# A gated delta rule in a four-stage program: decays scanned on VectorE, keys scaled on ScalarE, query norms folded into gating

## What is computed

```python
def step(S, inp):
    qt, kt, vt, gt, bt = inp
    S = S * jnp.exp(gt)
    delta = (vt - kt @ S) * bt
    S = S + kt[:, None] * delta[None, :]
    return (S, qt @ S)
...
q = short_conv(hidden_states @ Wq, conv_wq)
k = short_conv(hidden_states @ Wk, conv_wk)
q = l2norm(q.reshape(B, T, H, -1))
k = l2norm(k.reshape(B, T, H, -1))
beta = jax.nn.sigmoid(hidden_states @ Wb)
g = -jnp.exp(A_log) * jax.nn.softplus(hidden_states @ Wa + dt_bias)
o = gated_delta_rule(q, k, v, g, beta)
o_n = o * jax.lax.rsqrt(jnp.mean(o * o, axis=-1, keepdims=True) + NORM_EPS) * norm_w
o_n = o_n * jax.nn.silu(gg)
```

## Time and profile before

| | us |
|---|---|
| median of three runs | 1908.83 (1908.02 to 1911.7) |
| the profiled execution | 1907.61 |
| its span, first to last instruction | 1905.7 |
| delta rule within it | about 822 to 1644 |

### The profile page before, as it was taken

How to read it: one execution, slowest core, us unless ns; L and a number is a source line. 1 busy time by engine, 2 the same in 40 slices (tenths; PEclk the granted TensorE clock), 3 DMA queues, 4 the chain that set the end, 5 groups by cost and what they waited for, 6 DMA issues and landing times. The chain is left out here.

```text
span 1905.7 us, 27790 instructions
## 1 busy us (share of the span) xinstructions
PE 1526.6 (80%) x10592; PEld 1026.1 (54%) x10666; DVE 1038.4 (54%) x2369; ACT 665.9 (35%) x1185; POOL 693.8 (36%) x1097
## 2 busy tenths in 40 slices
PE   4787787777959996758799999999999996387782
PEld 3354554444536664324565676657666675365562
DVE  3856556455223553746467666777668542155553
ACT  3062251431612222544344544454444521022112
POOL 3020110300000000016778777787768672111343
PEclk8999899898979997989899999999999976598896
DMA  1000000000030003230231223222331211421355
GB/s 54 1 1 1 23 2 1 23 1 1 13 90 12 23 22 109 83 67 17 40 56 23 42 48 57 43 36 34 56 56 26 37 29 28 126 95 56 79 116 143
DMA packets 216902, 84.33 MB, mean 44 GB/s; under 512 B 166265, under 2 KB 211682, under 8 KB 216770
## 3 DMA queue, kind: packets, MB, share of 16 engines
q1 hardware_dynamic: 205330, 68.10, 16.1%
q0 software_dynamic: 5376, 12.59, 2.5%
q10 hardware_dynamic: 6064, 1.86, 0.4%
HBM read 50.80 MB, written 31.72 MB: 43 GB/s over the span
## 5 line engine op out<-in xcount | busy, mean ns | idle before, releaser
L1806 DVE SCALAR_TENSOR_TENSOR d_conv<-d_prep,k_cw,d_conv 128x511 f32<-128x511 f32 (+2 forms) x288 | 214.3, 746 | 32.1 <-ACT d_conv L1637 25.3
L1758 POOL TENSOR_TENSOR d_prod<-d_blk 64x30 f32<-64x30 f32 (+4 forms) x360 | 173.4, 482 | 102.9 <-DMA d_blk<-mid_a_blk 75.6
L1427 PE MATMUL d_prep<-k_hT,k_w 128*128 128x512 f32 x384 | 190.7, 621 | 24.4 <-POOL d_power L1732 12.7
L1762 POOL TENSOR_TENSOR d_blk<-d_blk,d_prod 64x30 f32<-64x30 f32 (+4 forms) x360 | 183.4, 509 | 28.2
L424 ACT ACTIVATE a_probs<-a_acc 128x896 f32<-128x896 f32 x128 | 117.1, 918 | 173.7 <-PE a_acc L248 110.7
L523 DVE TENSOR_REDUCE a_top<-a_turn 128x4 f32<-128x512 f32 (+3 forms) x240 | 147.5, 652 | 48.2 <-PE a_turn L210 40.4
L471 POOL TENSOR_TENSOR a_rstd<-a_rstd,a_mhalf 128x4 f32<-128x4 f32 x4 | 4.1, 1027 | 368.8 <-DVE a_rstd L575 368.8
L1427 PEld LDWEIGHTS d_prep<-k_hT,k_w 128*128 128x128 f32 x384 | 68.4, 198 | 85.6 <-issue 48.8
L1637 ACT ACTIVATE d_conv<-d_prep,k_cw 128x512 f32<-128x512 f32 x96 | 66.0, 687 | 132.6 <-PE d_prep L1427 132.4
L1465 PE MATMUL d_prep<-d_kq 128*128 128x256 f32 x384 | 94.7, 391 | 15.8 <-DVE d_qkT L1838 15.1
L1465 PEld LDWEIGHTS d_prep<-d_kq 128*128 128x128 f32 x384 | 72.8, 197 | 44.6 <-DVE d_qkT L1838 26.9
(11 more groups left out here) (356 smaller groups left out, 3522.5 us busy)
## 6 DMA issues: line engine op xcount, KB each, us to landing
mid_gate<-p_gate SPq DMA_DIRECT2D x4, 768.0 KB, 3.4
mid_v<-p_v_tok SPq DMA_DIRECT2D x4, 768.0 KB, 3.7
d_v_h<-mid_v SPq DMA_DIRECT2D x12, 256.0 KB, 5.6
d_gate_h<-mid_gate SPq DMA_DIRECT2D x12, 256.0 KB, 5.4
mid_a_blk<-d_AT SPq DMA_DIRECT2D x48, 64.0 KB, 2.0
d_blk<-mid_a_blk SPq DMA_DIRECT2D x12, 256.0 KB, 3.6
mid_u_blk<-d_blk SPq DMA_DIRECT2D x12, 256.0 KB, 2.9
mid_l_blk<-d_blkT SPq DMA_DIRECT2D x12, 256.0 KB, 3.7
```

The costliest lines, as they stand in the source:

```text
L1427: last = nc.tensor.matmul(PB[f % 2][:], w[:, n % 2, i, k, :], hT[:, k, b * T:(b + 1) * T], start=k == 0, stop=k == CK - 1)
L1758: nc.gpsimd.tensor_tensor(pr, blk[:, 0:t, t:t + 1].broadcast_to([lanes, t, m]), blk[:, t:t + 1, t + 1:BLK].broadcast_to([lanes, t, m]), AL ...
L1762: nc.gpsimd.tensor_tensor(blk[:, 0:t, t + 1:BLK], blk[:, 0:t, t + 1:BLK], pr, ALU.subtract).then_inc(subst, 1)
L1806: ins = nc.vector.scalar_tensor_tensor(dst, PB[f % 2][:, 0:T - j], cw[:, n % 2, f % 2, TAPS - 1 - j:TAPS - j], dst, ALU.mult, ALU.add)
```

## The change

- The decays from position to position are no longer made by matmuls and Exp. With exp(g) of each position, alpha, in a row, a scan along the row gives the running products: out[t] = out[t-1] x alpha[t] + diag[t], where `diag` is 1 on the diagonal and alpha is 0 at the first position of each chunk (which ends the row before). The projections turn g over on TensorE, raise it (`alpha_ready`) and store it; `load_decays` (SyncE) loads 512 alphas of one head and batch, the same row for all 128 partitions; `scan_decays` (VectorE) scans it in place, in the recurrence two heads ahead. `spread`, `differences`, `decay_up` and their constants and buffers go.
- `keep_keys` is on ScalarE, 16 copies of 128x128 with the decay as scale.
- The multiply by the query norms goes: mean(o^2) + eps |q|^2 takes the place of mean((o/|q|)^2) + eps, with `eps_q` made in `scales`. `raise_norms` has 16 columns instead of 32.
- The forming stands wholly ahead of the inversion on VectorE, queries first (`weigh_queries` of tiles 0 and 1 before the norms). On TensorE `turn_out` and `correlate(q, 0)` stand ahead of `sum_squares(q, 1)`. On ScalarE the last `keep_out` of a head stands ahead of the last Silu of the head two later. `scale_values` stands ahead of `finish`.
- `gate_h` has two buffers and its own load, later in SyncE's queue.

```diff
@@ layer1_projections @@
+                    if b - 2 == BATCH - 1:
+                        sp.wait_ge(alpha_ready, 1)
+                        sp.dma_start(d["alpha"].rearrange("(a r) t -> r a t", a=2), alpha[:]).then_inc(alpha_out, 16)
                     store_values(b - 2)
...
+            for a in range(2):
+                last = nc.tensor.transpose(GB[1][0:n // 2, 2 * P + a * P:2 * P + (a + 1) * P],
+                                           g[:].rearrange("p h t -> p (h t)")[:, a * (n // 2):(a + 1) * (n // 2)], ident[:])
             last.then_inc(summed, 1)
...
+            nc.scalar.activation(alpha[:, :, 1:P], GB[1][0:n // 2, 2 * P:4 * P].rearrange("r (a t) -> r a t", a=2)[:, :, 1:P], ACT.Exp).then_inc(alpha_ready, 1)
@@ layer1_delta_rule, SyncE @@
+            def load_decays(n, some):
+                for b in some:
+                    if n:
+                        sp.wait_ge(attn, 8 * n - 8 + 2 * b + 2)
+                    sp.dma_start(alpha[:, b, :], alpha_d[n:n + 1, b, :].broadcast_to([P, T])).then_inc(alpha_in[b], 16)
...
                 if n + 1 < D_H:
                     gather_blocks(n + 1)
+                if n + 3 < D_H:
+                    load_decays(n + 3, range(BATCH - 1))
                 if n + 2 < D_H:
                     spread_blocks(n + 2)
+                if n + 3 < D_H:
+                    load_decays(n + 3, range(BATCH - 1, BATCH))
                 store(n)
                 if n + 3 < D_H:
                     load_values(n + 3)
+                if n + 2 < D_H:
+                    load_gate(n + 2)
@@ TensorE, turn @@
-                if q < D_H:
-                    differences(q, 0)
                 if 0 <= m < D_H:
                     turn_keys(m, ORDER[:3])
-                if q < D_H:
-                    sum_squares(q, 1)
                 if 1 <= m:
                     turn_out(m - 1, CH - 1)
                 if q < D_H:
                     correlate(q, 0)
+                    sum_squares(q, 1)
                     correlate(q, 1)
                 if 0 <= m < D_H:
                     turn_keys(m, ORDER[3:])
                 if q < D_H:
                     turn_sums(q, 1)
-                    for b in range(1, BATCH):
-                        differences(q, b)
-                        correlate(q, 2 * b)
-                        correlate(q, 2 * b + 1)
+                    for f in range(2, 8):
+                        correlate(q, f)
@@ ScalarE @@
                 if f == 7:
+                    if n >= 2:
+                        keep_out(n - 2, CH - 1)
                     silu(n, 7)
                     square(n, 3)
...
+            def keep_keys(n, i):
+                b = ORDER[i]
+                act.wait_ge(k_turned, BATCH * n + i + 1)
+                for c in range(CH):
+                    t = b * CH + c
+                    ins = nc.scalar.activation(k_tok[:, t, :], LB[b][:, c, :], ACT.Copy, scale=decays[:, 1, n, t:t + 1])
+                ins.then_inc(k_ready, 1)
...
                 if q < D_H:
-                    decay_up(q, 0)
                     keep_sums(q, 1)
-                    for b in range(1, BATCH):
-                        decay_up(q, b)
                 if 0 <= m < D_H:
+                    for i in range(BATCH):
+                        keep_keys(m, i)
@@ VectorE @@
             def scales(n):
                 dve.wait_ge(n_half, 2 * n + 2)
+                nc.vector.tensor_scalar(eps_q[:, n % 3, :], norm2[:, 1, :], EPS_RMS, None, ALU.mult)
...
+            def scan_decays(n):
+                for b in range(BATCH):
+                    dve.wait_ge(alpha_in[b], 16 * n + 16)
+                    nc.vector.tensor_tensor_scan(alpha[:, b, :], alpha[:, b, :], diag[:], 0.0, ALU.mult, ALU.add).then_inc(decayed, 1)
...
                         nc.vector.tensor_copy(R[:], r_src).then_inc(r_ready, 1)
+                    if ahead and c == 0:
+                        scan_decays(n + 2)
                     dve.wait_ge(solved, CH * n + c + 1)
...
-                nc.vector.tensor_tensor(o[:], o[:], vec(norm[:, n % 2, 1, :]), ALU.mult).then_inc(rchain, 1)
...
-                nc.vector.tensor_scalar(mean2[:], mean2[:], 1.0 / D_V, EPS_RMS, ALU.mult, ALU.add).then_inc(mean_ready, 1)
+                nc.vector.scalar_tensor_tensor(mean2[:], mean2[:], 1.0 / D_V, eps_q[:, n % 3, :], ALU.mult, ALU.add).then_inc(mean_ready, 1)
...
                 if q < D_H:
+                    if q < 2:
+                        scan_decays(q)
+                    weigh_queries(q, 0)
+                    weigh_queries(q, 1)
                     take_sums(q, 1)
                     scales(q)
...
+                    weigh_keys(q, 0)
+                    weigh_keys(q, 1)
+                    for f in range(2, 8):
+                        weigh_queries(q, f)
+                        weigh_keys(q, f)
+                    scale_values(q)
                 if n >= 0:
                     finish(n)
```

More of the change, by code:

```diff
@@ L951, in delta_constants @@
     out["c_after"] = (i[:, None] > i[None, :]).astype(np.float32)
-    out["c_past"] = in_bf16(np.repeat(np.where(i[:, None] <= i[None, :], 0.0, NEG)[:, None, :], CH, 1))
+    out["c_diag"] = np.tile(np.eye(P, dtype=np.float32), (1, CH))
     return out
@@ L1021, in _ @@
             load_x(3)
[L1022 to L1023 removed]
+            sp.dma_start(kept.diag[:], d["c_diag"]).then_inc(kept_in, 16)
             for n in range(2):
@@ L1394, in store @@
                 sp.dma_start(o_d[n, :, :, :], o_out[:]).then_inc(stored, 16)
+            load_decays(0, range(BATCH))
             for n in range(3):
                 load_values(n)
+            for n in range(2):
+                load_gate(n)
+            load_decays(1, range(BATCH - 1))
             spread_blocks(0)
+            load_decays(1, range(BATCH - 1, BATCH))
             load_weights(2)
             gather_blocks(0)
+            load_decays(2, range(BATCH - 1))
             spread_blocks(1)
+            load_decays(2, range(BATCH - 1, BATCH))
             for n in range(D_H):
@@ L1445, in turn_sums @@
                 last.then_inc(n_turned, 1)
-            def differences(n, b):
-                pe.wait_ge(gu_ready, BATCH * n + b + 1)
-                if b or n:
-                    pe.wait_ge(decayed, BATCH * n + b)
-                if b == 0 and n >= 2:
-                    pe.wait_ge(fs_ready, (CH - 1) * (n - 1))
-                nc.tensor.matmul(DB[:], after[:], g_upto[:, b % 2, :, :].rearrange("p c t -> p (c t)"), start=True, stop=False)
-                nc.tensor.matmul(DB[:], identb[:], past[:].rearrange("p c t -> p (c t)"), start=False, stop=True).then_inc(diff, 1)
             def correlate(n, f):
@@ L1670, in recur @@
                         convolve(n + 2, 2 * c + 1)
-                keep_out(n, CH - 1)
+                if not ahead:
+                    keep_out(n, CH - 1)
             def prepare(n):
@@ L1844, in scale_values @@
                     .then_inc(nchain, 1)
                 dve.wait_ge(nchain, 2 * n + 2)
-            def keep_keys(n, start, end):
-                for i in range(start, end):
-                    b = ORDER[i]
-                    dve.wait_ge(k_turned, BATCH * n + i + 1)
-                    dec = decays[:, 1, n, b * CH:(b + 1) * CH]
-                    nc.vector.tensor_tensor(k_tok[:, rows[b], :], LB[b][:], dec[:, :, None].broadcast_to([P, CH, P]), ALU.mult).then_inc(k_ready, 1)
             def keep_l(n, i):
```

135 lines of the change are left out of this document (51 added, 84 removed).

## The result

The changed kernel takes 1902.97 us (median of 20 runs, 1897.92 to 1909.25) against 1909.3 us for the kernel before (20 runs, 1901.21 to 1916.39). The ratio is 0.9967, 95% interval 0.9956 to 0.9977: 6.3 us faster, where I had forecast 18.5. The profiled execution of after is the slowest of its 20 (1909.25 us, span 1907.3), so it can't be set against that of before as a whole. It is already 5.3 us late when the delta rule begins, with a first instruction of the stage at 828.34 us against 823.08; in the traces of the nine kernels built from after that follow here, the same point lies between 823.2 and 827.2. Intervals within the stage are what can be compared.

What follows compares the result with a forecast made beforehand. TensorE looked like the bound before; then the block loop, 45.8 + 1.5 + 7.3 + 0.5 + 4.0 = 59.1 us a head, would exceed TensorE's 57.4. Gain 18.5 us, giving 1890 us; range 1866 to 1908.

Steps and rivals of the forecast that it cites:

- TensorE loop: Delta rule, per head: recurrence, forming of head n+2, inversion of head n+1; to fall from 60.6 to 57.4 us.
- Norms: In the forming on VectorE, after the row sums of squares: to start at 1157.25 instead of 1158.51, 1.25 us earlier.
- The pairs: Forming, pairs 2 to 7 of `correlate` and VectorE's product: 2.2 us for two, before 2.8 to 3.2.
- Rival 2: Forming shortens by no more than 1 us, VectorE being the pairs' slower partner; TensorE loop 59.5, about 1900 us; chance 0.08.
- A of head 0: Moment when head 0's diagonal-block stores are issued: from 871.0 to 869.1, forming gaining 2.6 us, projections costing 0.7.
- Keys on ScalarE: 16 key copies on ScalarE, 4.2 to 5.6 us per head, hidden by the forming.
- The scan at 1.2 us: Each 128x512 scan on VectorE, nearest the 0.70 us two-operand pass; four take 4.8 us and fit the gap before `eps`.
- Rival 3: Long scans make it slower than before: near 1923 us at 2.0 us each, near 1990 at 3.6; chance 0.12.
- The port stall of 4.0 us: VectorE scans and `gate_out`, reading two SBUF tensors, hold up GpSimd's substitution: 3.5 plus 0.5 us a head.
- Rival 1: Port costs nothing or scans miss the substitution; block loop 55.1, TensorE binds at 57.4; 1871 us, chance 0.27.
- the block loop: Per head: block stores, reload, GpSimd substitution, SyncE's return, inversion of the next turn; to bind at 59.1 us.
- the one on SyncE: Three decay loads ahead of the block stores: 1.5 us of issues, plus 0 to 3 us delay to stores, taken as 0.5.

Runs made afterwards that it cites:

- the two edits: Changed kernel with the decay loads moved behind the block stores and the scans' second operand in PSUM: 1870.46 us, ratio 0.9792; run again 1870.03 us.
- the PSUM run: Changed kernel with the scans' second operand in PSUM, each scan split in two, decay loads still ahead of the block stores: 1874.98 us, ratio 0.9813.
- the loads-behind run: Changed kernel with all four decay loads put behind the block stores and the reload of the blocks in SyncE's queue: 1891.01 us, ratio 0.9911.

## Why the prediction was right or wrong

**The sign, the bound and the likeliest case were right, the size was not.** Point by point:

- TensorE loop 60.6 to 57.4: right. Norms were to come 1.25 us earlier after the square and came 1.6 earlier (4.20 instead of 5.82 in every head from the third on). The pairs were forecast at 2.2 us and take 2.16. Uncovered by the two edits, the loop measures 57.0. Rival 2 is out.
- The head of the stage: A of head 0 was to gain 2.6 and gained 2.2 us, measured from the stage's start.
- Keys on ScalarE, hidden: right, 4.24 us for 16 copies, between the sums and the inversion.
- The scan at 1.2 us, taken from the lower row: right, 1.2 to 1.65, median 1.26. It fits into VectorE's gap, which still has 2.5 to 3.3 us left. Rival 3 is out. The Trainium skill's rule of half throughput, in "DVE: opcode table, instruction layouts, handler registers and perf-mode slots", section 6, agrees roughly: 1.26 us against 0.69 for a plain product of this size.
- The port stall of 4.0 us on the substitution: right in place and size (37.6 to 41.6), and shown by the PSUM run to be that. Rival 1, at 1871, was the kernel without the stall and with the loads where they are. That is the PSUM run, and it measures 1875: the store delay is in it. The 1870 of both edits, without that delay, is what rival 1's sum describes.
- That the bound moves to the block loop: right. The inversion is released by the DMA of `L` in 11 heads, where it had been two, the first and the last.
- **The step that failed** is the one on SyncE: "Their 768 KB go ahead of these stores through the same engines ... at the least it is nothing ... I take 0.5." The stores took 2.0 us longer to their reload (5.5 instead of 3.5; landing 3.4 instead of 2.0). 1.5 us over ten heads are 15 us, and the interval from the second to the last start is 15.2 us longer than forecast. The range of 0 to 3 was right and I took its cheap end, arguing that most of the load would be done before A. With the block loop binding, the first three batches' `attn` are ready when SyncE gets to the loads: all three are issued in 1.44 us without a wait, and the stores follow 1.6 us after the first. The argument used the timing of a forming that is waited for; that was no longer so. The PSUM run, where the forming is waited for again in the later heads, has both timings side by side, with the same loads ahead (stores and reload of the fifth and of the ninth head):

```profile
1100.92 2.31 SPq L1397 DMA_DIRECT2D mid_a_blk<-d_AT  x4
1107.60 0.47 SPq L1400 DMA_DIRECT2D d_blk<-mid_a_blk  x1
...
1334.31 1.95 SPq L1397 DMA_DIRECT2D mid_a_blk<-d_AT  x4
1338.00 0.47 SPq L1400 DMA_DIRECT2D d_blk<-mid_a_blk  x1
```

  In the fifth head the last load is issued 0.5 us ahead of the stores and the reload follows them by 6.7 us; in the ninth 2.0 us ahead, and 3.7. Of the seven heads with 1.5 us or more ahead, five have 3.5 to 4.0 us and two 4.9; the three with less have 5.1 to 6.7. So the cheap end was the right price for the timing that I had assumed.
- The same step missed at head 1: from its stores to its reload are 5.2 us and from there to GpSimd's start 4.7 (4.7 and 3.8 before), 9.9 together, where the sum had 7.8. The second start came 2.0 us later than before, relative to the stage's start, instead of the 0.2 forecast. That is 1.8 us; smaller differences of A and of the first substitution, both ways, make up the balance.
- Together 17 us would leave 1.5 of 18.5. The stage as a whole is 3.0 us shorter (818.39 against 821.37), the medians differ by 6.3. Of the 1.5 us that the stage gains beyond the sum's, 1.1 are GpSimd's last substitution, which is over before `gate_out` has got far (37.5 us instead of 38.6). The last 3 us, outside the stage, I can't place: the two profiled executions lie at different points of their spreads of 11 and 15 us.
- Not in the sum at all: the granted clock. That the bound moves to the block loop was forecast; that TensorE, waiting, then begins seven of ten inversions at 0.5 was not. What it costs in after the runs do not separate.

## What to carry to other kernels

When a change makes a loop shorter, ask again for every queue which transfers now meet: a wait that used to hold a transfer back until the road was free has gone. Put loads that nobody waits for behind the stores that somebody waits for, and count a transfer in front by what it takes when both are issued together, unless something else still holds the store back. If a heavily used engine starts to wait, look at the granted clock behind the waits. If VectorE must work beside GpSimd, give one of its operands a place in PSUM before asking how long its passes are.

## What the runs showed of the hardware

- Stores of 64 KB issued right behind three loads of 256 KB on the same queue land after 3.4 us instead of 2.0 (medians of after and of the loads-behind run). With the last load issued 1.5 to 2.2 us ahead, in the PSUM run, the reload follows the stores after 3.5 to 4.0 us in five heads and after 4.9 in two, where it is 3.5 without loads ahead.
- The stall between VectorE and GpSimd works in both directions. I had counted GpSimd's loss only; in the forming shown first a `gate_out` pass over 128x512, 0.69 us alone, took 2.12 beside a GpSimd pass of 1.99 (the longest of its twelve in after):

```profile
1222.55 1.99 POOL L1780 TENSOR_SCALAR d_blkT<-d_blk 64x1024 f32<-64x1024 f32 x1
1222.81 2.12 DVE L1918 TENSOR_TENSOR d_o_out<-d_o 128x512 f32<-128x512 f32 x1
```

- A scan costs 1.2 us for 512 elements with both operands in SBUF, and 0.66 for 256 with the second in PSUM; a head's scans take 4.6 and 4.7 us. A GpSimd step beside it takes its own time if that operand is in PSUM, and nearly the scan's (1.03 to 1.10 us) if it is not.
- In after TensorE has waited 2.1 to 4.5 us for `L` in seven of the ten heads in between, and each time its granted clock is 0.5 (1.2 GHz) for 3.4 to 6.1 us of the work that follows. With both edits, where it waits 2.2 us at most, it is 1.00 from 929 to 1512 us.
